# A six-layer graph-attention kernel: orders within its period changed, and its beginning laid out anew

## The reference

```python
# layer 0
q, k, v = ((x @ W + b).reshape(b_, n, 8, 32) for W, b in ((Wq, bq), (Wk, bk), (Wv, bv)))
attn = softmax(where(adj == 0, -inf, einsum('bnhd,bmhd->bhnm', q, k) * scale))
y = einsum('bhnm,bmhd->bnhd', attn, v).reshape(b_, n, d) @ Wo + bo + x
x = (y - mean(y)) * rsqrt(var(y) + eps) * gamma + beta
# layer 1
w = softmax(where(adj == 0, -inf, (x @ Wq) @ (x @ Wk).T * scale))
x = layer_norm(x + (w @ (x @ Wv)) @ Wo + bo)
# layers 2 to 5
attn = where(mask, 0, softmax(where(mask, -1e10, (x @ Wq.T + bq) @ (x @ Wk.T + bk).T / sqrt(128))))
x = layer_norm(x + (attn @ x) @ Wc.T)
```

## Time and profile before

| what | us |
|---|---|
| median of 3 runs | 2533.27 (2532.14 to 2534.21) |
| the profiled execution's own time | 2531.23 |
| span of that execution, first to last instruction | 2529.4 |
| TensorE busy | 2382.8 (94%) |
| GpSimd busy | 1841.4 (73%) |
| ScalarE busy | 1570.5 (62%) |
| VectorE busy | 1553.4 (61%) |

### The profile page before, as it was taken

The page is one execution under the profiler, slowest core; times in us unless marked ns, Lnnn a source line. Parts: engine busy times, 40 slices in busy tenths (PEclk is TensorE's granted clock), DMA queues, the critical chain, the costliest instruction groups (busy, mean ns, idle before and its releaser), DMA issues.

```text
span 2529.4 us, 57112 instructions
## 1 busy us (share of the span) xinstructions
PE 2382.8 (94%) x20944; PEld 2182.5 (86%) x20944; DVE 1553.4 (61%) x4874; ACT 1570.5 (62%) x5512; POOL 1841.4 (73%) x2439
## 2 busy tenths in 40 slices
PE   5899999999999999999999999999999999999985
PEld 4789889889889889889889889889888888888874
DVE  2566666666666666666666666666666666666663
ACT  4666666666666666666666666666656656656642
POOL 3577777777777777777777777777777777777773
PEclk8999999999999999999999999999999999999997
DMA  3000000000000000000000000000000000000000
GB/s 141 22 26 22 24 31 22 25 30 20 27 31 18 28 31 18 28 31 18 29 30 18 28 30 18 28 30 18 28 31 18 29 31 18 28 31 12 14 10 13
DMA packets 38150, 68.62 MB, mean 27 GB/s; under 512 B 4336, under 2 KB 12656, under 8 KB 37232
## 3 DMA queue, kind: packets, MB, share of 16 engines
q1 hardware_dynamic: 37872, 64.97, 7.5%
HBM read 48.18 MB, written 16.78 MB: 26 GB/s over the span
## 4 chain that ended last, share of the span: by engine, by line
PE 58%; DVE 13%; ACT 12%; POOL 12%; issue 3%; DMA 0%; DVEq 0%; SPq 0%; POOLq 0%
PE qk_bank L374 12%; PE value_bank L382 11%; ACT probs L607 8%; PE unit_bank L374 7%; PE context_bank L527 6%; PE unit_bank L437 4%; POOL rstd L909 4%; PE qk_bank L480 4%; PE unit_bank L382 4%; DVE xT_lo L771 4%; POOL x_out L928 3%; POOL x_out L930 3%; PE unit_bank L449 3%; DVE y L825 2%; DVE y L806 2%
## 5 line engine op out<-in xcount | busy, mean ns | idle before, releaser
L928 POOL TENSOR_TENSOR x<-y,rows 128x512 f32<-128x512 f32 x320 | 407.9, 1275 | 280.2 <-DVE y L825 280.2
L825 DVE TENSOR_SCALAR y<-y,mv,rstd 128x256 f32<-128x256 f32 x768 | 280.7, 408 | 362.1 <-POOL rstd L909 362.0
L627 ACT CAST xT_hi<-qk_bank 128x512 fp32r<-128x512 f32 x320 | 191.2, 598 | 449.7 <-PE qk_bank L480 449.7
L374 PE MATMUL qk_bank<-xT_hi,w_lo 128*128 128x256 f32 x1280 | 405.4, 317 | 67.0 <-DVE xT_lo L771 67.0
L930 POOL TENSOR_TENSOR x<-x,rows 128x512 f32<-128x512 f32 x320 | 412.5, 1289 | 25.1
L607 ACT ACTIVATE probs<-unit_bank,negmax 128x128 f32<-128x128 f32 x1024 | 366.0, 384 | 49.9 <-DVE negmax L743 49.9
L382 PE MATMUL value_bank<-w_lo,xT_hi 128*128 128x256 f32 x1280 | 393.1, 307 | 0.0
L806 DVE SCALAR_TENSOR_TENSOR y<-context_bank,rtotal,x 128x256 f32<-128x256 f32 x640 | 277.2, 474 | 155.6 <-PE context_bank L527 155.6
L374 PE MATMUL qk_bank<-xT_lo,w_hi 128*128 128x256 f32 x1280 | 361.7, 283 | 0.0
L382 PE MATMUL value_bank<-w_hi,xT_lo 128*128 128x256 f32 x1280 | 361.6, 283 | 0.0
L374 PE MATMUL qk_bank<-xT_hi,w_hi 128*128 128x256 f32 x1280 | 360.5, 282 | 0.0
(11 more groups left out here) (89 smaller groups left out, 6339.1 us busy)
## 6 DMA issues: line engine op xcount, KB each, us to landing
x0T<-xT_in SPq DMA_DIRECT2D x64, 256.0 KB, 2.6
x<-x_in SPq DMA_DIRECT2D x64, 256.0 KB, 2.6
out<-x_out SPq DMA_DIRECT2D x64, 256.0 KB, 2.1
adj<-adj_in SPq DMA_DIRECT2D x64, 128.0 KB, 2.2
rows<-rows_in SPq DMA_DIRECT2D x1, 1920.0 KB, 11.4
probs0T<-w_in SPq DMA_DIRECT2D x1, 1024.0 KB, 5.1
probs<-w_in SPq DMA_DIRECT2D x1, 1024.0 KB, 8.1
x<-w_in SPq DMA_DIRECT2D x1, 1024.0 KB, 14.0
```

The costliest lines, as they stand in the source:

```text
L374: mm = pe.matmul(psum[:, n * G * N:(n + 1) * G * N], split(w, name, kd, at, at + P), flat(xT_half[:, kd]), start=kd == 0 and w is w_lo, st ...
L825: m = dve.tensor_scalar(y[:, r, g], y[:, r, g], mv[:, r, g, 0:1], rstd[:, r, g:g + 1], ALU.subtract, ALU.mult)
L928: pool.tensor_tensor(new, y[:, r], row_of_each(f"gamma{layer}"), ALU.mult).then_inc(zg_ready, 1)
```

## The change

1. **ScalarE.** A period's four `exp0` stood so: unit 0 early and unit 1 at the end of slot 4, unit 2 early in slot 0, unit 3 in slot 1. Now unit 1 stands early in slot 0, and unit 2 at its end. `move_v` of slot 0 goes from ahead of the `exp0` to behind it.
2. **GpSimd.** `scale_and_shift` is cut into `scale` and `shift`. In slot 3 the group's `find_rstd` comes between the item's `scale` and `shift`. In slot 0 `normalise_probs0` of unit 1 goes behind the item's `find_rstd`.
3. **VectorE.** `reciprocal0` of unit 1 goes behind the item's statistics.
4. **Beginning.** `x0T` of group 0 is loaded first, then wv0, wq0 and wk0 in a transfer each, each with its own semaphore and its own split; `wo0` goes straight to its tile; of `rows` only `bv0` is loaded early; `eye` and `adj` come earlier. The loads get semaphores of their own. `fuse_layer1` moves from slot -7 to slot -6, behind `score0` of group 0, and its splits from slot -7 to slot -5. Chunk 3 is loaded only in slot -3, since chunk 1 is staged in its tile.
5. **Late weights.** Layers 2 to 5 are split a layer at a time, in slots 1, 5, 9 and 13, with the low part on VectorE instead of GpSimd.

```diff
+FIRST_WEIGHTS = ["wv0", "wq0", "wk0"]
+LATER_SLOTS = [STEP * (layer - 1) for layer in range(2, LAYERS)]
+LATER_LEAD = 3
...
-            sp.dma_start(cols[:, :], cols_in).then_inc(first_loaded, 16)
-            load_chunk(0, first_loaded)
             load_x0T(0)
-            load_chunk(1, rest_loaded)
-            sp.dma_start(rows[:, :, :], rows_in.partition_broadcast(P)).then_inc(rest_loaded, 16)
-            sp.dma_start(eye[:, :], eye_in).then_inc(rest_loaded, 16)
+            for name in FIRST_WEIGHTS:
+                sp.dma_start(staged(0)[:, first_weight(name)], w_in[:, first_weight(name)]).then_inc(w0_loaded[name], 16)
+                if name == FIRST_WEIGHTS[0]:
+                    sp.dma_start(cols[:, :], cols_in).then_inc(cols_loaded, 16)
+            sp.dma_start(eye[:, :], eye_in).then_inc(eye_loaded, 16)
             load_adj(0)
+            sp.dma_start(rows[:, 0:1, :], rows_in[0:1].partition_broadcast(P)).then_inc(bv0_loaded, 16)
+            sp.dma_start(flat(wo0[:, :]), w_in[:, first_weight("wo0")]).then_inc(wo0_loaded, 16)
             load_x0T(1)
-            load_chunk(2, later_loaded[0])
+            load_chunk(1, w1_loaded)
             load_x0(0)
-            load_chunk(3, later_loaded[1])
+            sp.dma_start(rows[:, 1:, :], rows_in[1:].partition_broadcast(P)).then_inc(rows_loaded, 16)
...
             for i in SLOTS:
+                if i == -3:
+                    sp.wait_ge(fused_in_psum, 2)
+                    load_chunk(3, later_loaded[1])
...
@@ tensor
-                if i == -7:
+                if i == -6:
                     fuse_layer1()
...
@@ scalar
+                if i == FIRST:
+                    for name in FIRST_WEIGHTS:
+                        split_first(name)
                 if item(i - 1):
                     softmax(i - 1)
-                if item(i - 1) and late_values(i - 1):
-                    move_v(i - 1)
                 if (group := due(i, 6)) is not None:
                     exp0(group, 0)
                 if (group := due(i, 5)) is not None:
-                    exp0(group, 2)
+                    exp0(group, 1)
...
+                if item(i - 1) and late_values(i - 1):
+                    move_v(i - 1)
                 if item(i):
                     move_qk(i)
                 if item(i - 1):
                     move_probsT(i - 1)
-                if (group := due(i, 6)) is not None:
-                    exp0(group, 1)
+                if (group := due(i, 5)) is not None:
+                    exp0(group, 2)
...
-                if i in (-5, -4):
-                    split_later(i + 5)
+                if i + LATER_LEAD in LATER_SLOTS:
+                    split_later(LATER_SLOTS.index(i + LATER_LEAD))
...
@@ vector
                     row_max0(group, 2)
-                    reciprocal0(group, 1)
...
                 if (group := due(i, 5)) is not None:
+                    reciprocal0(group, 1)
                     row_max0(group, 3)
...
+                if i + LATER_LEAD in LATER_SLOTS:
+                    n = LATER_SLOTS.index(i + LATER_LEAD)
+                    dve.wait_ge(later_hi_ready, n + 1)
+                    split_weight(later_at[n], LATER, later_staged(n)).then_inc(later_lo_ready, 1)
...
@@ gpsimd
                 if (group := due(i, 5)) is not None:
                     normalise_probs0(group, 0)
-                    normalise_probs0(group, 1)
...
                 if item(i - 2):
                     find_rstd(("item", i - 2))
+                if (group := due(i, 5)) is not None:
+                    normalise_probs0(group, 1)
                 if item(i - 1):
                     keep_valid(i - 1)
                 if item(i - 2):
-                    scale_and_shift(("item", i - 2))
+                    scale(("item", i - 2))
                 if (group := due(i, 2)) is not None:
                     find_rstd(("group", group))
-                    scale_and_shift(("group", group))
+                if item(i - 2):
+                    shift(("item", i - 2))
+                if (group := due(i, 2)) is not None:
+                    scale(("group", group))
+                    shift(("group", group))
```

107 lines of the change are left out of this document (61 added, 46 removed).

## The result

| | median | lowest to highest | ratio to before, 95% interval |
|---|---|---|---|
| before | 2532.9 us | 2532.1 to 2534.2 | |
| changed | 2491.7 us | 2491.1 to 2492.3 | 0.9837 (0.9820 to 0.9854) |

The change makes the kernel 41 us faster. The forecast was 2440, with a range from 2413 to 2470: it is missed, by 52 us, on the side of rival (a).

A forecast was written before the change was run, and what follows sets the result against it. TensorE, 94% busy, was taken as the bound, with waits in slots 4 and 0. 1.36 a period over 59 periods (80.2), beginning 12.3 and net 1.0 made 93.5 off 2531.2; plus 2.0, 2440 us, range 2413 to 2470.

The forecast's parts named there:

- rival (a): Slot 4: GpSimd's item addition and VectorE's group `normalise` block each other, 0.88 turns to -0.2 a period, 2503 us; chance 8%.
- What bounds the kernel, and where TensorE stands: TensorE, 94% busy, bounds the kernel; its three waits per period are all in slots 4 and 0.
- Slot 4, 0.88 a period: Group's `rstd` no longer behind the item's shift, so `context` to transposition falls from 4.46 to 3.58 us.
- specimen, slot 14: Early slot with no item in GpSimd's slot 13; its 3.58 us from `context` to transposition gave slot 4's forecast.
- the row at 1005.67: VectorE `normalise` starting inside a 0.19 us GpSimd instruction without delay, at its usual 0.74; cited against mutual blocking.
- Slot 0, 0.48 a period: Time from transposition to first product of `project_v` falls from 4.93 to 4.45 us.
- The wait for the copy of `v`: Slot 0: TensorE's `project_v` newly waits some 0.3 us for ScalarE's copy, now behind unit 1's exponentials.
- The beginning, 12.3: Start of the kernel: earlier first product, layer 1's products moved behind `score0` and smaller casts save 12.3 us, bounds 10 to 15.
- the late splits, -2.5: Filling: the four late weight splits on ScalarE and VectorE cost 2.5 us, at worst 8.8, at best nothing.
- Slots 5, 10 and 15, +2.5: These slots have slot 0's wait and gain about 0.5 to 1.1 us each, 2.5 together.
- Slot 314, +1.0: In the emptying, TensorE's 2.07 us wait for `xT_lo` behind the group's `normalise` gets 1.0 back.
- What would show it: Signs in the new trace, such as 36.7 us between `score0` starts; a late-starting slot 4 `normalise` would point to mutual blocking.

The follow-up runs named there:

- e1_group_scale_first: The changed kernel with the group's scale moved ahead of the item's shift in GpSimd's slot 3; 2452.6 us, ratio 0.9676.
- m1_sum_written_out: The changed kernel with the group's `normalise` on VectorE also writing out a sum of each row, order kept; 2452.4 us, ratio 0.9678.
- e8_v_as_before: The changed kernel with slot 0's copy of `v` put back ahead of unit 1's exponentials on ScalarE; 2475.1 us, ratio 0.9772.
- e3_beginning_only: The changed kernel with the period's orders on ScalarE, VectorE and GpSimd as before, only beginning and late weights new; 2524.8 us, ratio 0.9962.

## Why the prediction was wrong, point by point

- **What bounds the kernel, and where TensorE stands**: right. The two places named, slots 4 and 0, are the two that moved, and slots 1 to 3 stayed within 0.07.
- **Slot 4, 0.88 a period**: the step that failed. "The group's variance can now be worked on at about 1016.06 [...]: all that follows on VectorE comes 1.01 sooner." `rstd` did come 1.0 sooner, but `normalise` did not end sooner: 0.07 of 0.88 was left, and 0.81 x 59 = 48 of the 52 us were missing. The step took "all that follows" for granted, that is, it put the overlap of `normalise` with GpSimd's shift at nothing: it costs 0.94 (1.67 in place of 0.73). Its specimen, slot 14, lacked the very instruction that the change put beside `normalise`. With that instruction out of the way (`e1_group_scale_first`) the specimen's 3.58 holds exactly.
- **Rival (a), 8%**: right in its mechanism, shown by `m1_sum_written_out`, at 2503 a little too dear. It had `normalise` held for a full 1.27, to come at 1018.3, and slot 4 at -0.2. In fact the first instruction was lengthened by 0.94, and slot 4 gained 0.07. What was weighed against it was the row at 1005.67, beside a GpSimd instruction of 128x2 elements that was over 0.12 later (1005.60 + 0.19); a hold could not have been longer than that. It said nothing about an instruction of 1.27, and should not have outweighed the row for it, 1.63 in place of 1.3.
- **Slot 0, 0.48 a period**: right, 0.50 measured (6.88 to 6.38; from the transposition to the first value product 4.93 to 4.42). The wait for the copy of `v` was forecast at 0.3; having the copy behind unit 1's exponentials costs 0.25 (`e8_v_as_before`). The prediction named it as a cost of the change and did not draw the conclusion that this part of the change should be the other way round.
- **The beginning, 12.3, and the late splits, -2.5**: both mis-sized, with errors that partly offset each other. First product at 6.60 (6.1 forecast), group 0's scores at 13.94 (13.7), 14.35 ahead at group 1, where 12.3 was forecast: the higher clock, which the prediction had only as its upper bound, is worth 2.45. Then 4.0 is given back, 3.3 of it by the late splits. With the old orders (`e3_beginning_only`) 8 to 9 us are left of the forecast's 9.8. That this is close is in part luck: the forecast was 2.1 too low at the start, and 0.8 too low in what the splits cost.
- **Slots 5, 10 and 15, +2.5**: too much. Slot 5's bracket fell from 1.10 to 0.63, slot 10's went from 0.50 to 0.55, and slot 15's of 0.50 is gone. From group 1 to group 5 the changed kernel takes 135.4 and `e3_beginning_only`, with the old orders and the same splits, 136.1: all new orders together bring about 0.6 there. **Slot 314, +1.0**: wrong, by the same step as slot 4. TensorE waits as long as before, 2.07, and its `normalise` runs beside the item's shift (TensorE in slots 5 and 314, then VectorE and GpSimd in slot 314 of the changed kernel):

```profile
70.38 0.39 PE L395 MATMUL qk_bank<-xT_hi,w_lo 128*128 128x256 f32 x1 [0.63 <-DVE xT_lo L804]
...
2384.52 0.39 PE L395 MATMUL qk_bank<-xT_hi,w_lo 128*128 128x256 f32 x1 [2.07 <-DVE xT_lo L804]
```

```profile
2381.87 1.66 DVE L860 TENSOR_SCALAR y<-y,mv,rstd 128x256 f32<-128x256 f32 x2 [1.14 <-POOL rstd L951]
```

```profile
2381.80 1.26 POOL L975 TENSOR_TENSOR x_out<-x_out,rows 128x512 f32<-128x512 f32 x1
```

- **What would show it**: "a `normalise` in slot 4 that starts well behind its `rstd` (a)". It starts on time and lasts long; a reader who looked for a bracket would have missed it.

## What to carry to other kernels

When an order on GpSimd is changed, ask of each of its long instructions what VectorE will run beside it: here a `tensor_scalar` in SBUF was held by it, and the hold was no bracket but a longer duration, found in the mean of its group. A specimen from another part of the trace is worth what its neighbours are worth: check that what the change puts beside the instruction is beside it there too. Where two waits follow each other in a ring of engines, the second grows when the first goes, so measure the edits together as well as singly (39 and 17 gave 64).

## What the runs showed of the hardware

- VectorE's `tensor_scalar` on 128x256 fp32, SBUF to SBUF: 0.41 by itself (the group mean before is 408 ns), 1.35 when a GpSimd addition of 1.27 had begun 0.07 earlier; with the sum written out 0.54, and not held.
- In the changed kernel `xT_lo`, a VectorE subtraction with one operand in PSUM, ran beside GpSimd's scale at its usual time (at 1035.22, 0.67, beside a scale from 1035.04 to 1036.31). With both operands in SBUF and begun 0.2 earlier, VectorE's subtraction of 128x1024 stretched GpSimd's 128x512 instruction, 1.27 by itself, to 2.26 (an addition) and 2.19 (a scale).
- On GpSimd a 128x512 instruction that needs the one before it starts 1.35 behind it, an independent one 1.23 (changed kernel, 1035.04 and 1036.39; `e1_group_scale_first`, 1018.23 and 1019.46).
- TensorE's products of 128x256 took 0.41 us at a granted clock of 0.50 (from 34 to 38 us in the kernel before) and 0.28 at 1.00 (from 22.8 to 26.2 in the changed kernel). The first products of both kernels took 0.41 as well (in the changed kernel up to 10.3), though the record gives 1.00 there.
